# Second attention's output weight: loaded at the head of the expert stage, scaled 32 columns at a time inside its loop

## The reference, cut to what matters

```
mod = (_silu(L1_c) @ L1_wmod).reshape(L1_c.shape[0], 6, 1, -1)
sa, ca, ga, sb, cb, gb = (mod[:, 0], mod[:, 1], mod[:, 2], mod[:, 3], mod[:, 4], mod[:, 5])
ga = (2 * (ga >= 0) - 1) * jnp.maximum(jnp.abs(ga), 0.25)
...
x = x + ga * _L1_attn_ref(h, L1_attn_Wq, L1_attn_bq, L1_attn_Wkv, L1_attn_bkv, L1_attn_Wo, L1_attn_bo)
```

## Time and profile before

| | us |
|---|---|
| median of 3 runs | 2205.89 |
| lowest and highest | 2197.26, 2205.98 |
| the profiled execution, its time | 2209.23 |
| the profiled execution, its span in the trace | 2207.4 |

### The profile page before, as it was taken

The page is one execution under the profiler, slowest core; times in us unless marked ns, Lnnn a source line. Parts: engine busy times, 40 slices in busy tenths (PEclk is TensorE's granted clock), DMA queues, the critical chain, the costliest instruction groups (busy, mean ns, idle before and its releaser), DMA issues. The chain is left out here.

```text
span 2207.4 us, 38661 instructions
## 1 busy us (share of the span) xinstructions
PE 2005.0 (91%) x11188; PEld 1316.5 (60%) x11189; DVE 1000.2 (45%) x3238; ACT 742.6 (34%) x1747; POOL 732.1 (33%) x668
## 2 busy tenths in 40 slices
PE   4799869799999999999999389999849999999998
PEld 1666645455555555555555256566528878788787
DVE  2367658334466422222222266676534453443432
ACT  0233327222222222222222067777713333223221
POOL 1144420345555555545554454544121101011000
PEclk8799979999999999999999689999979999999999
DMA  6222523598878888888887211100012121121220
GB/s 233 101 70 71 200 70 101 123 227 201 206 182 194 194 196 210 219 212 196 203 219 176 79 34 32 33 4 4 1 49 67 63 82 58 59 84 62 81 67 19
DMA packets 107128, 258.55 MB, mean 117 GB/s; under 512 B 25488, under 2 KB 29200, under 8 KB 106896
## 3 DMA queue, kind: packets, MB, share of 16 engines
q1 hardware_dynamic: 68240, 163.61, 23.4%
q0 software_dynamic: 35552, 88.63, 19.8%
q10 hardware_dynamic: 3232, 4.95, 0.6%
HBM read 196.55 MB, written 59.54 MB: 116 GB/s over the span
## 5 line engine op out<-in xcount | busy, mean ns | idle before, releaser
L1238 PE MATMUL bank<-arena 128*128 x1272 | 440.3, 489 | 2.1 <-ACT arena L1279 0.9
L1191 POOL DMA_INDIRECT x_sum<-route,arena x158 | 254.4, 1610 | 184.2 <-DVE route L1355 158.9
L1238 PEld LDWEIGHTS bank<-arena 128*128 128x128 f32 x1272 | 229.9, 191 | 134.6 <-issue 8.9
L1255 PE MATMUL bank<-arena 96*128 x632 | 298.9, 595 | 2.1 <-issue 2.0
L1202 POOL DMA_INDIRECT arena<-h_moe,arena x158 | 155.6, 985 | 223.9 <-DVE arena L1349 216.9
L1929 PE MATMUL bank<-x_hi,w_hi 128*128 128x512 f32 x512 | 201.0, 392 | 6.0 <-DVE x_lo L2062 6.0
L1342 DVE SCALAR_TENSOR_TENSOR arena<-arena,bank 128x192 f32<-128x192 f32 x159 | 66.0, 415 | 309.4 <-ACT arena L1274 309.4
L1929 PE MATMUL bank<-x_hi,w_lo 128*128 128x512 f32 x512 | 199.5, 390 | 0.0
L1929 PE MATMUL bank<-x_lo,w_hi 128*128 128x512 f32 x512 | 199.3, 389 | 0.0
L1274 ACT ACTIVATE arena<-bank 128x192 f32<-128x192 f32 x159 | 52.8, 332 | 361.0 <-PE bank L1238 361.0
L1255 PEld LDWEIGHTS bank<-arena 96*128 96x128 f32 x632 | 107.3, 190 | 81.2 <-issue 81.1
(11 more groups left out here) (329 smaller groups left out, 3498.0 us busy)
## 6 DMA issues: line engine op xcount, KB each, us to landing
arena<-in_moe_up SPq DMA_DIRECT2D x64, 768.0 KB, 6.3
ffn_arena<-in_ffn_up SPq DMA_DIRECT2D x64, 512.0 KB, 3.3
arena<-in_moe_down SPq DMA_DIRECT2D x64, 384.0 KB, 7.8
arena<-in_L_wmod SPq DMA_DIRECT2D x12, 1024.0 KB, 6.9
x_sum<-route SPq DMA_DIRECT2D x18, 256.0 KB, 2.8
x_res<-in_L_attn_x SPq DMA_DIRECT2D x1, 4096.0 KB, 18.5
h_moe<-arena SPq DMA_DIRECT2D x16, 256.0 KB, 2.1
x_sum<-x_res SPq DMA_DIRECT2D x16, 256.0 KB, 2.4
```

Source lines behind the costliest of these rows:

```text
L1191: nc.gpsimd.indirect_dma_start(out=x_sum[b], out_offset=bass.IndirectOffsetOnAxis(ap=st_dst[:, b], axis=0), in_=y[:, b], in_offset=None, c ...
L1238: mm = nc.tensor.matmul(psum[2 + b][:, 0:2 * FI], xgT[:, b, k], up_ring[:, bass.ds((e % RING) * UPW + k * 2 * FI, 2 * FI)], start=(k == 0) ...
L1255: mm = nc.tensor.matmul(psum[6 + b][:], hiddenT[:, b, n], down_ring[:, bass.ds((e % RING) * DOWNW + n * C, C)], start=(n == 0), stop=(n == 1))
```

## The change

The five DMAs for `wo` and `bo` move from behind SP's ring loop to its head, behind the load of the fourth expert, with a semaphore of their own, `wo_in`. DVE waits for it between its first loop and its second. A new function `scale_wo(n)` scales 32 columns of `wo` and is called at the end of each of the 15 passes of the second loop, with n from 0 to 14, and for n = 15 behind the last turn. There `bo` is still scaled. `sel` and `spread` are built ahead of `finish_mod` at the stage's head. `DVE_W` grows from 9 to 10.

```
@@ sync engine @@
                 load(AHEAD, AHEAD)
+                wo_rows = a["L1_attn_Wo"].rearrange("(c r d) n -> c d r n", c=NKV1, r=HP)
+                for c in range(NKV1):
+                    sp.dma_start(later1.wo[HD * c:HD * c + HD], wo_rows[c]).then_inc(wo_in, 16)
+                sp.dma_start(later1.bo, a["L1_attn_bo"].partition_broadcast(P)).then_inc(wo_in, 16)
                 with sp.Fori(1, E // RING) as n:
...
                 landed(32 * E // RING, RING - 1)
-                wo_rows = a["L1_attn_Wo"].rearrange("(c r d) n -> c d r n", c=NKV1, r=HP)
-                for c in range(NKV1):
-                    sp.dma_start(later1.wo[HD * c:HD * c + HD], wo_rows[c]).then_inc(late_in, 16)
-                sp.dma_start(later1.bo, a["L1_attn_bo"].partition_broadcast(P)).then_inc(late_in, 16)
@@ vector engine, the loops @@
                     st.end(NT - 1)
+                    dve.wait_ge(wo_in, 16 * N_WO)
                     with dve.Fori(NT, SURE) as i:
...
                         transform_high(n)
+                        scale_wo(n)
                     st.end(NT - 1)
 
+                def scale_wo(n):
+                    x = later1.wo[:, :, n * COLS:n * COLS + COLS] if isinstance(n, int) else later1.wo[:, :, bass.ds(n * COLS, COLS)]
+                    gate = cols(mod[:, 1, 2], n)
+                    st.did(tt(x, x, gate.unsqueeze(1).to_broadcast([P, HP, COLS]), ALU.mult))
+
+                st.did(nc.vector.tensor_copy(later1.sel.rearrange("n r (c d) -> n r c d", c=NKV1),
...
+                st.did(nc.vector.tensor_copy(later1.spread.rearrange("p (h k) -> p h k", h=HM),
...
                 finish_mod(NT - 1)
...
                 schedule(dve, turn, sure=sure)
 
-                wo, bo = later1.wo, later1.bo
-                dve.wait_ge(late_in, 16 * N_LATE)
-                st.did(tt(wo[:], wo[:], mod[:, 1, 2].unsqueeze(1).to_broadcast([P, HP, C]), ALU.mult))
-                st.did(tt(bo, bo, mod[:, 1, 2], ALU.mult))
-                st.did(nc.vector.tensor_copy(later1.sel.rearrange("n r (c d) -> n r c d", c=NKV1),
...
-                st.did(nc.vector.tensor_copy(later1.spread.rearrange("p (h k) -> p h k", h=HM),
...
+                scale_wo(NT - 1)
+                st.did(tt(later1.bo, later1.bo, mod[:, 1, 2], ALU.mult))
                 st.settle()
```

More of the change, by code:

```diff
@@ L46 @@
 GN = GT * P
-DVE_M, DVE_W = 12, 9
+DVE_M, DVE_W = 12, 10
 DVE_F = 21
@@ L1120, in adaln_two_layers @@
             w_read, slots_known, rows_known = psem("m_w_read"), psem("m_slots_known"), psem("m_rows_known")
-            late_in = psem("m_late_in")
-            N_LATE = 11
+            late_in, wo_in = psem("m_late_in"), psem("m_wo_in")
+            N_LATE, N_WO = 6, 5
             def schedule(eng, turn, steps=None, per=0, sure=None):
@@ L1369, in sure @@
                         transform_high(n)
+                        scale_wo(n)
                     st.end(NT - 1)
+                def scale_wo(n):
[3 more added lines that the diff above has]
+                st.did(nc.vector.tensor_copy(later1.sel.rearrange("n r (c d) -> n r c d", c=NKV1),
+                                             ident[0:NHEAD, 0:NHEAD].rearrange("n (c r) -> n r c", r=HP).unsqueeze(3).to_broadcast([NHEAD, HP, NKV1, HD])))
+                st.did(nc.vector.tensor_copy(later1.spread.rearrange("p (h k) -> p h k", h=HM),
+                                             ident[0:META, 0:META].unsqueeze(1).to_broadcast([META, HM, META])))
                 finish_mod(NT - 1)
@@ L1376, in _ @@
                 schedule(dve, turn, sure=sure)
-                wo, bo = later1.wo, later1.bo
-                dve.wait_ge(late_in, 16 * N_LATE)
-                st.did(tt(wo[:], wo[:], mod[:, 1, 2].unsqueeze(1).to_broadcast([P, HP, C]), ALU.mult))
-                st.did(tt(bo, bo, mod[:, 1, 2], ALU.mult))
-                st.did(nc.vector.tensor_copy(later1.sel.rearrange("n r (c d) -> n r c d", c=NKV1),
-                                             ident[0:NHEAD, 0:NHEAD].rearrange("n (c r) -> n r c", r=HP).unsqueeze(3).to_broadcast([NHEAD, HP, NKV1, HD])))
-                st.did(nc.vector.tensor_copy(later1.spread.rearrange("p (h k) -> p h k", h=HM),
-                                             ident[0:META, 0:META].unsqueeze(1).to_broadcast([META, HM, META])))
+                scale_wo(NT - 1)
+                st.did(tt(later1.bo, later1.bo, mod[:, 1, 2], ALU.mult))
                 st.settle()
```

## The result

| | before | changed |
|---|---|---|
| median, us | 2206.07 | 2210.40 |
| lowest and highest of 22 runs, us | 2197.26, 2214.31 | 2206.57, 2218.39 |
| profiled execution: its time, its span, us | 2209.23, 2207.4 | 2215.61, 2213.8 |

The ratio of the times is 1.0024, with a 95% interval of 1.0014 to 1.0034: the changed kernel is slower by 5.3 us (3.1 to 7.5). The two medians alone differ by 4.3 us, which lies inside that interval. The forecast was 2206.0, no change. 2210.4 lies inside the stated range of 2197 to 2211, but the loss is real, and it wasn't the likeliest case.

The account below looks back on a forecast made before the run. PE was taken to bound the stage, and POOL's DRAIN to close its end. Terms -0.3 + 0.5 + 0.1 - 0.2 = +0.1 us on the 2205.89 median gave 2206.0, no change (0.60); range 2197 to 2211.

Parts of the forecast that it names:

- The head: Stage's head: five loads beside the first gather, which PE waits for, cost +0.5 us, within 0 to 3.0.
- The end: Stage's end: DVE is done 2.5 us earlier, but POOL's own DRAIN closes the stage; -0.3 us.
- The drag of 12%: Stage's end: DVE's work slows POOL's by some 12%, so 2.5 us less of it gives 0.3 us.
- The first rival: Stage's end: POOL's DRAIN follows DVE and shrinks, so the whole 2.5 us come back; 2203.8 us, chance 0.25.
- The second loop: DVE's second loop: the added multiplication fits into sequencer time, L1342 comes 0.1 to 0.15 us later; +0.1 for 15 passes.
- The second rival: Second loop: DVE's sequencer can't run ahead, L1342 starts 0.61 us later and holds PE; 4.6 us, 2210.5, chance 0.08.
- The old place of the loads: Where the loads stood before: five of eleven DMAs leave a stretch with PE idle 0.66 us; -0.2 us.
- `sel` and `spread`: Stage's head: they cost DVE 0.6 us, hidden in its 1.20 us wait for the first gather.
- full head cost: Stage's head: the loads cost the full 3.0 us, the longest landing of 30 gathers; 2208.5 us, chance 0.07.
- PE's wait at the head: Sign at the stage's head: PE's wait for the first gather stays between 8.4 and 9 us.
- The next phase: Sign at the stage's end: it starts under 0.6 us behind POOL's DRAIN, still some 4.6 us long.
- The stage's length from the first matmul to the last scaling: Sign over the expert stage: a change of over 3 us would make the forecast wrong.

Follow-up runs that it names:

- e1: Kernel before with only the five `wo` and `bo` loads moved to the stage's head; ratio to the kernel before 1.0019.
- e2: Changed kernel with SP starting the five loads only after PE has transposed the first two tiles; ratio to the kernel before 1.0008.
- e3: Changed kernel with the fourth expert's load held until the first tile is transposed and `wo`'s parts each one tile later; ratio to the kernel before 0.9997.
- e4: e2 with one more POOL DRAIN between the last scatters and the wait for their landing; ratio 1.0007.
- e7: e3 with one more POOL DRAIN behind POOL's loop, ahead of the last two scatters; ratio to the kernel before 0.9996.
- e6: e3 with the old scaling, all of `wo` behind the last turn and nothing in the loop; ratio 0.9987.
- e13: Kernel before with the 1.0 MB `Wq` load, one DMA over 128 partitions, moved to the stage's head; 8.41 us from gather to matmul.
- e9: Changed kernel with the five loads started by ACT instead of SP; one time, 2217.18 us.
- e10: Changed kernel with two of `wo`'s four parts at the head, the other two and `bo` held until the gather is through; 2209.06 us.
- e11: Changed kernel with `bo` alone at the head and all of `wo` behind PE's second transposed tile; 2209.28 us.
- e14: Changed kernel with SP waiting, before the five loads, for POOL's count for its second gather; 9.48 us from gather to matmul.
- e5_before_again: Kernel before, unchanged, profiled a second time; 813.1 us from first matmul to last scaling.

## Why the prediction was wrong, step by step

**The head, the step that failed.** The term for the loads at the head was +0.5 us, and it measured +4.9 to +6.3. The prediction put the loads in PE's wait for the first gather, which was the right place, and asked how long that gather could take. It took +0.5 and bounded it at +3.0 by the longest of 30 landings, 8.1 us. The profile of the changed kernel has +6.3, and e1 +4.9. The term was mis-sized, beyond its upper bound. The error is in the choice of the bounding rows. Those 30 gathers ran at a DMA share of 0.82 with 192 GB/s, and not beside 1.25 MB more in a queue, mostly in a narrow form. The same group of rows held a warning that went unused for this purpose: the `wo` loads themselves took 4.9 to 8.5 us to land. If the loads go ahead of the gather or share the engines with it, the gather can come nearly as late as the last of them. Both happened: no packet of the gather for 6 us, then equal shares, and a landing 1.8 us ahead of the last part of `wo`. The measured +4.9 to +6.3 against a total of +5.3 (3.1 to 7.5) leaves little for anything else, and the four kernels that take the collision away (e2, e3, e4, e7) come back to the time before within 2 us.

The prediction drew on the Trainium skill (DMA: Bandwidth & Descriptors, Queues, rings and completion order), by which each DMA engine takes turns between its queues packet by packet, and read it to mean that a deeper queue would cost the gather nothing. The runs don't bear that reading out: 11.46 us against 5.15 with 1.25 MB more in SP's queue, and 8.93 with them in ACT's. From the gather's first packet on, the even shares of q0 and q1 in the changed kernel agree with taking turns. The 6 us ahead of it, in which q0 moves nothing, the reading left out.

**The end, right.** POOL's DRAIN closes the stage, it is its own work, and DVE's 2.5 us lay under it. The forecast was -0.3. The one profile shows -0.56, but single profiles scatter: the five with the whole scaling at the end and no DRAIN or work added (the two of before, e1, e6, e13) have ends of 14.55, 14.57, 14.31, 14.38 and 14.24, mean 14.41; the seven with the change's end (changed, e2, e3, e9, e10, e11, e14) have 13.99, 14.39, 14.35, 14.75, 14.32, 14.40 and 14.12, mean 14.33. So the gain is 0.1 us on average. The drag of 12% that was argued from the scatters isn't seen in the DRAIN, which has 4638 ns with 2.3 us more of DVE's late work and with 2.5 us less. The first rival, with a chance of 0.25, is refuted by that; the contention that the prediction cited from the Trainium skill (GPSIMD Engine Reference, Specifications) had no effect on the DRAIN.

**The second loop, right in its step, open in its sum.** L1332 to L1342 grew from 1.32 to 1.46 us, and 1.4 to 1.5 was forecast. The second rival, L1342 late by 0.61, didn't come. PE's busy share there was forecast as 98 to 99% and is 149.09 of 155.00 us in the changed kernel, 96%. But 149.20 is found in e1 too, which has no scaling in the loop, 153.43 in e7, which has it, and 150.66 in e5_before_again, against 152.81 in the first profile of the same kernel. In the changed kernel the two largest rows of PE's waits in that stretch don't name L1342:

```profile
PE bank L1255 <- issue: 2.6, 4, 1.0
PE bank L1247 <- DMA arena<-h_moe,arena: 2.4, 2, 1.2
```

(us in total, times, longest; e1, without the scaling, has 2.5 and 2.4 in the same two rows.) For the 30 tiles under that loop, nine profiles with the scaling in it have a mean of 158.1 us (standard deviation 2.0), seven without it 156.2 (1.7). The difference is 1.9 us with a 95% interval of about 0 to 4, where +0.1 was forecast. The profiles differ in other things too, and e6 against e3, the one comparison by whole times, is too coarse. So a second term may have been too small by 2 us or so; it isn't shown.

**The old place of the loads, too small to tell.** Forecast -0.2, measured -0.3 in its window, in which kernels with the loads at the old place differ by 0.9 among themselves.

**`sel` and `spread`, right.** They are in the changed kernel and not in e1, and both have the long wait; DVE still waits 7.04 us for the gather, and 1.0 us in e2, where the gather isn't held.

**The chances.** A loss of 0.24% lies in "same" by the bound of 0.5%, and in the range, which came from the scatter of single runs. With 22 runs each the medians tell 0.1% apart, so the expected scatter hid from the forecast that a loss of 5 us is measurable; the rival "full head cost" had 0.07, and the head's true price lay beyond even that.

**The signs that the prediction named.** PE's wait at the head, 8.4 to 9 us, was the one that failed (14.66). The next phase was to start under 0.6 us behind POOL's DRAIN; it started 0.8 behind it, but so it did in the kernel before (1224.04 to 1224.83), so this sign was misread from the rows. The stage's length from the first matmul to the last scaling changed by 2.9 us (810.6 to 813.5), just under the 3 that would have counted against the forecast; as two profiles of the kernel before differ by 2.5, it tells nothing.

**What stays open.** Why the gather moves no packet for some 6 us while SP's or ACT's queue has loads: e9, e10 and e14 show that it is so whichever of the two queues holds them and also for loads issued during the gather's instruction, but not by what rule. Whether the narrow form costs more by its 32 partitions or by being several DMAs. And what POOL's first DRAIN does in its 4.64 us.

## What to carry to other kernels

Before you move a load to "an idle place", look for the one small transfer that the bound engine is waiting for there: the load is sure to cost nothing there only if it starts behind that transfer's landing (e2, e3), not merely behind its start (e14), and its price isn't bounded by how long such transfers take elsewhere, but by the landing of the load itself. A profile's DMA rows by queue show directly when the small transfer's packets move. Work taken off the engine that finishes second to last at a barrier gains nothing; find the DRAIN that ends last, and test whether its length reacts to what you mean to remove. Loads that can be held by one wait until the first tile is in should be.

## What the runs showed of the hardware

- A gather of 128 rows, started by POOL, took 3.80 us to PE's first use with nothing beside it, 5.0 to 5.4 beside a 1.15 MB load, 5.50 with 0.25 MB more over 128 partitions, 8.41 with 1.0 MB more in one DMA over 128 partitions, 9.32 with 0.5 MB more in two DMAs over 32 partitions, 9.5 to 11.5 with all five from SP, and 8.93 with them from ACT.
- While loads ran in SP's or ACT's queue, the gather's first packet came 5.7 to 6.2 us behind its start (changed, e1, e9, e10, e14), 2.75 in the kernel before, and 1.9 with nothing beside it (e3). After that, POOL's queue and SP's had equal shares in the changed kernel (49.9% and 55.9%).
- Loads to 32 partitions kept the DMA engines at a share of 1.06 to 1.07 with 169 to 187 GB/s (e10, changed); loads to 128 partitions had 291 to 294 at 0.95 to 1.05 (e13, e11).
- The first DRAIN of POOL behind a stage with hundreds of its DMAs takes 4638 ns, the same in every kernel that left it at the barrier; 4467 when it stands ahead of the last two scatters, and then 0.22 at the barrier. Issued ahead of the scatters' landing, it took 10.83 us and ended 4.4 behind their last packet (e4).
- POOL raised the count for its second gather at 387.03, 0.25 us ahead of the start of its first (e14): what an engine's sequencer signals ahead of an instruction doesn't say that the one before it has started.
